# Where a kernel's scattered rows are issued, when its expert tiles start, and how far attention outputs are buffered

## The reference, cut to what matters

```python
x = x + tanh(g_xattn[0]) * xattn(layernorm(x), ctx, ctx, Wq, bq, Wk, bk, Wv, bv, Wo, bo, mask)
x = x + tanh(g_ffn[0]) * ffn(layernorm(x), gate_w, gate_b, w1, b1, w2, b2)
# xattn: softmax(q k^T / sqrt(8), masked) v, then @ Wo.T + bo
# ffn:
scores = x_flat @ gate_w + gate_b
topk_vals, topk_idx = top_k(scores, 2)
topk_probs = softmax(topk_vals)
combine_w = zeros((T, 8)).at[tok, topk_idx].add(topk_probs)
h = relu(einsum('td,edf->etf', x_flat, w1) + b1[:, None, :])
y = einsum('etf,efd->etd', h, w2) + b2[:, None, :]
out = einsum('te,etd->td', combine_w, y)
```

## Time and profile before

| | us |
|---|---|
| median of 3 runs | 507.41 (505.67 to 509.38) |
| the profiled execution | 506.01 |
| its span, first to last instruction | 504.2 |

### The profile page before, as it was taken

How to read it: one execution, slowest core, us unless ns; L and a number is a source line. 1 busy time by engine, 2 the same in 40 slices (tenths; PEclk the granted TensorE clock), 3 DMA queues, 4 the chain that set the end, 5 groups by cost and what they waited for, 6 DMA issues and landing times.

```text
span 504.2 us, 12347 instructions
## 1 busy us (share of the span) xinstructions
PE 418.4 (83%) x4299; PEld 333.3 (66%) x4299; DVE 268.6 (53%) x1010; ACT 284.4 (56%) x848; POOL 271.8 (54%) x297
## 2 busy tenths in 40 slices
PE   0779889999899999998988777988589999999900
PEld 0455667667667667576756466977479899999800
DVE  1345667777677676776667553433422333233247
ACT  1277868778787778786856711423133444444334
POOL 8536319059498496793942801864755355554500
PEclk9979999999999999999989956998879999999965
DMA  3999999500000000000010052555538677778278
GB/s 74 240 359 410 412 392 216 104 12 14 23 12 23 25 12 23 13 13 29 8 33 14 33 179 81 175 167 168 173 117 251 197 218 233 239 217 247 90 231 280
DMA packets 48155, 72.55 MB, mean 144 GB/s; under 512 B 8054, under 2 KB 32638, under 8 KB 48094
## 3 DMA queue, kind: packets, MB, share of 16 engines
q1 hardware_dynamic: 43549, 62.32, 40.6%
q0 software_dynamic: 4544, 9.45, 5.3%
HBM read 41.83 MB, written 34.66 MB: 152 GB/s over the span
## 4 chain that ended last, share of the span: by engine, by line
PE 74%; issue 8%; DVE 5%; DMA 4%; ACT 3%; SPq 3%; POOL 1%; another core or an unknown queue 1%; DVEq 0%; POOLq 0%; ACTq 0%
PE S L740 7%; PE T L718 7%; PE O L740 7%; PE U L718 7%; PE S L624 6%; PE O L664 6%; PE O L654 6%; PE T L632 6%; PE S L614 5%; PE U L632 5%; ACT P L819 2%; DMA yg<-res 2%; DVE PT L1074 2%; PE E L673 2%; PE E L688 2%
## 5 line engine op out<-in xcount | busy, mean ns | idle before, releaser
L819 ACT ACTIVATE P<-S,nmax 128x120 f32<-128x120 f32 x512 | 135.2, 420 | 6.9 <-DVE nmax L1068 5.4
L959 POOL DMA_INDIRECT zs<-z,posu x64 | 63.2, 988 | 99.6 <-DVE posu L1147 81.0
L970 POOL DMA_INDIRECT res<-yo,dpos x78 | 75.0, 961 | 64.7 <-DVE yo L1231 56.6
L1068 DVE TENSOR_REDUCE nmax<-S 128x4 f32<-128x480 f32 x128 | 75.1, 649 | 37.4 <-PE S L624 32.3
L826 ACT COPY PT<-U 120x512 f32<-120x512 f32 x64 | 39.6, 619 | 52.9 <-PE U L632 51.7
L856 ACT ACTIVATE H<-T,wbuf 128x256 f32<-128x256 f32 x78 | 32.7, 471 | 62.5 <-PE T L718 45.0
L614 PE MATMUL S<-mb_r,I_r 128*128 128x480 f32 x128 | 65.3, 514 | 2.1 <-ACT P L819 1.9
L856 ACT ACTIVATE H<-U,wbuf 128x256 f32<-128x256 f32 x78 | 32.7, 471 | 51.7 <-PE U L718 37.3
L938 POOL TENSOR_SCALAR Kb<-Kt,hm 128x480 f32<-128x480 f32 x32 | 47.0, 1482 | 18.2 <-ACT Kt L840 18.2
L928 POOL TENSOR_SCALAR z<-X,mv,rstd 128x128 f32<-128x128 f32 x64 | 50.2, 791 | 3.0 <-POOL rstd L923 2.7
L1080 DVE RECIPROCAL orec<-O 128x128 f32<-128x128 f32 x32 | 30.6, 957 | 39.2 <-PE O L664 39.2
(11 more groups left out here) (161 smaller groups left out, 654.0 us busy)
## 6 DMA issues: line engine op xcount, KB each, us to landing
wbuf<-wpk SPq DMA_DIRECT2D x39, 578.0 KB
zs<-zero SPq DMA_DIRECT2D x1, 17952.0 KB, 60.2
zin<-zs SPq DMA_DIRECT2D x39, 132.0 KB
yg<-res SPq DMA_DIRECT2D x16, 256.0 KB, 4.2
wpk<-in_w SPq DMA_DIRECT2D x1, 2048.0 KB, 57.7
wpk<-in_w SPq DMA_DIRECT2D x8, 256.0 KB, 9.3
out<-X SPq DMA_DIRECT2D x16, 128.0 KB, 3.4
ctx_sb<-in_ctx SPq DMA_DIRECT2D x1, 1440.0 KB, 16.8
```

The costliest lines, as they stand in the source:

```text
L819: ins = nc.scalar.activation(P[:, n % 4, j, :], a[:, j * LK:(j + 1) * LK], ACT.Exp, bias=nmax[:, n % 4, j:j + 1])
L959: nc.gpsimd.indirect_dma_start(out=zs, out_offset=bass.IndirectOffsetOnAxis(ap=posu[:, F, k, i:i + 1], axis=0), in_=z2[:, F % 2, i, :], in ...
L970: nc.gpsimd.indirect_dma_start(out=res, out_offset=bass.IndirectOffsetOnAxis(ap=dpos[:, n % NDP, h:h + 1], axis=0), in_=yo[:, n % NYO, h, ...
L1068: v.tensor_reduce(nmax[:, n % 4, :], Sb[n % NHG][:, 0:HG * LK].rearrange("p (j k) -> p j k", j=HG), AX_X, ALU.max, negate=True).then_inc(m ...
```

## The change

- `SCATTERS` issues a group's eight scatters as four at p = 1 and four at p = 3, both of group G - 2; none goes to the group after. Each part waits until the sums of batch k - 1 are done (`behind_sums`).
- From group 6 on, and for every scatter to `res`, a scatter also waits for `yo` number 4t/5 - 1, t being its turn (`paced`). Group 6's are issued in rounds 33 to 36, and the norm of `z2` for group 7 in round 33 instead of 34.
- Routing parts 4 and 5 stand ahead of the unload, part 2 of the table in round p = 2 instead of 3.
- `OT` has two buffers, `NYO` is 10.
- The steps of the tiles start in round 32, the opening steps at the end of round 31.
- SP loads tiles' rows and weights in turn, rows first; the wait for the table moves to the rows.

```diff
--- before.py
+++ after.py
@@ -35,8 +35,8 @@
 FIRST = ("Z", "C", "K", "Q", "V")
 
 
-SCATTERS = {0: (-3, (2, 3)), 1: (-2, (0,)), 2: (-2, ()), 3: (-2, (1,))}
-LAST_SCATTERS = {0: (), 1: (0,), 2: (1, 2), 3: (3,)}
+SCATTERS = {0: (-2, ()), 1: (-2, (0, 1)), 2: (-2, ()), 3: (-2, (2, 3))}
+LAST_SCATTERS = {0: (), 1: (0, 1), 2: (2,), 3: (3,)}
 
 
 
@@ -66,7 +66,7 @@
 NTAB = 13
 
 ZW, Z_TOK, Z_EXP = D + 4, D, D + 1
-NYO = 6
+NYO = 10
 NDP = NYO + 4
 
 TRASH = 2 + NDP * TS
@@ -94,7 +94,7 @@
 
     subs, pre, k = {}, {}, 0
     for b in range(NB):
-        j, k = 0, max(k, GB * (LAST[b] + 1) + 5)
+        j, k = 0, max(k, GB * (LAST[b] + 1) + 4)
         if k < NR:
             pre[k - 1] = b
         while j < SUBS[b] and k < NR:
@@ -304,7 +304,7 @@
         P = sb("P", [128, 4, HG, LK])
         PT = sb("PT", [LK, NPT, HG * LQ])
         orec = sb("orec", [128, LQ])
-        OT = sb("OT", [128, TOK])
+        OT = sb("OT", [128, 2, TOK])
         xb = sb("xb", [128, GB, D])
 
         z2T = sb("z2T", [128, TOK])
@@ -511,8 +511,6 @@
             def load_w(n):
 
                 b, i = tile_of(n)
-                if i == 0:
-                    sp.wait_ge(table_step, NTAB * (b + 1))
                 wait(sp, yo_done, TH * (n - NW + 1))
                 e = sp.value_load(tab[0:1, b, 1, i:i + 1], min_val=0, max_val=NE - 1)
                 sp.dma_start(wbuf[:, n % NW, :], wpk[bass.ds(e, 1)].squeeze(0)).then_inc(w_in[n % NW], 16)
@@ -521,6 +519,7 @@
 
                 b, i = tile_of(n)
                 if i == 0:
+                    sp.wait_ge(table_step, NTAB * (b + 1))
                     for q in range(2):
                         sp.wait_ge(scat[q], 16 * 2 * GB * ((LAST[b] + 1 - q) // 2))
                 if n >= NZ:
@@ -550,12 +549,13 @@
                     known = N0[b + 1]
                     if b + 1 < NB and ROUND_OF.get((b, 2 * TH * (i + 1) - 1), NEVER) > GB * (LAST[b + 1] + 1) + 1:
                         known = N0[b + 2]
-                    while w_next < min(N0[b] + i + NW, known):
-                        load_w(w_next)
-                        w_next += 1
-                    while z_next < min(N0[b] + i + NZ, known):
-                        load_z(z_next)
-                        z_next += 1
+                    while z_next < min(N0[b] + i + NZ, known) or w_next < min(N0[b] + i + NW, known):
+                        if z_next < min(N0[b] + i + NZ, known):
+                            load_z(z_next)
+                            z_next += 1
+                        if w_next < min(N0[b] + i + NW, known):
+                            load_w(w_next)
+                            w_next += 1
             stored(sp, N0[NB])
             for u in range(NU):
                 load_results(u)
@@ -670,7 +670,7 @@
                 a = entry("PROJ", G)
                 pe.wait_ge(o_free, at(G, GB, GB) + 1)
                 for i in range(GB):
-                    last = mm(a[:, i * D:(i + 1) * D], OT[:, i * LQ:(i + 1) * LQ], wo_sb[:], start=True, stop=True)
+                    last = mm(a[:, i * D:(i + 1) * D], OT[:, G % 2, i * LQ:(i + 1) * LQ], wo_sb[:], start=True, stop=True)
                 last.then_inc(e_ready, 1)
 
             def z2_entry(F):
@@ -945,6 +945,18 @@
                 nc.gpsimd.tensor_tensor(xb[:], group_x(G), bo_sb[:].unsqueeze(1).broadcast_to((128, GB, D)),
                                         ALU.add).then_inc(xb_done, 1)
 
+            def behind_sums(k):
+
+                if 1 <= k <= B:
+                    pool.wait_ge(pv_done, k)
+
+            turn = {"next": 0}
+
+            def paced():
+
+                turn["next"] += 1
+                return (turn["next"] - 1) * 4 // 5 - 1
+
             def scatter(F, part, parts):
 
                 if part == 0:
@@ -956,6 +968,8 @@
                     for k in range(2):
                         if (2 * i + k) * parts // (2 * GB) != part:
                             continue
+                        if F >= SB0[1]:
+                            wait(pool, yo_done, paced())
                         nc.gpsimd.indirect_dma_start(
                             out=zs, out_offset=bass.IndirectOffsetOnAxis(ap=posu[:, F, k, i:i + 1], axis=0),
                             in_=z2[:, F % 2, i, :], in_offset=None).then_inc(scat[F % 2], 16)
@@ -966,7 +980,7 @@
                 if q is None:
                     return
                 n, h = N0[b] + q // TH, q % TH
-                pool.wait_ge(yo_done, TH * N0[b] + q + 1)
+                pool.wait_ge(yo_done, max(TH * N0[b] + q + 1, paced()))
                 nc.gpsimd.indirect_dma_start(
                     out=res, out_offset=bass.IndirectOffsetOnAxis(ap=dpos[:, n % NDP, h:h + 1], axis=0),
                     in_=yo[:, n % NYO, h, :], in_offset=None).then_inc(y_out[n % NYO], 16)
@@ -974,17 +988,21 @@
             def round_(k):
                 G, p = divmod(k, GB)
                 F, parts = SCATTERS[p]
-                if 0 <= G + F < NG and G + F + 1 not in LAST:
+                if 0 <= G + F < NG and G + F + 1 not in LAST and k <= B:
                     for part in parts:
+                        behind_sums(k)
                         scatter(G + F, part, GB)
-                if p == 2 and 0 <= G - 1 < NG:
+                if p == (2 if G < NG else 1) and 0 <= G - 1 < NG:
                     pool.wait_ge(ln2_step, at(G - 1, 2, 2))
                     rstd(mv2, rstd2, rstd2_done, G - 1)
                     if G >= 3:
                         pool.wait_ge(scat[(G - 1) % 2], 16 * 2 * GB * ((G - 1) // 2))
                     normalise(z2[:, (G - 1) % 2, :, 0:D], G - 1, mv2, rstd2, z2_done, rstd2_done)
+                if B < k <= B + GB:
+                    scatter(NG - 2, k - B - 1, GB)
                 if G - 1 in LAST:
                     for part in LAST_SCATTERS[p] if G < NG else range(GB) if p == 1 else ():
+                        behind_sums(k)
                         scatter(G - 2, part, GB)
                 if p == 2 and G + 1 < NG:
                     masked_keys(G + 1)
@@ -1079,9 +1097,9 @@
                 G, i = divmod(k, GB)
                 v.reciprocal(orec[:], Ob[:, LQ:2 * LQ]).then_inc(orec_done, 1)
                 dve.wait_ge(orec_done, k + 1)
-                if i == 0 and G >= 1:
-                    ready(dve, "PROJ", G - 1)
-                v.tensor_tensor(OT[:, i * LQ:(i + 1) * LQ], Ob[:, 0:LQ], orec[:], ALU.mult).then_inc(o_free, 1)
+                if i == 0 and G >= 2:
+                    ready(dve, "PROJ", G - 2)
+                v.tensor_tensor(OT[:, G % 2, i * LQ:(i + 1) * LQ], Ob[:, 0:LQ], orec[:], ALU.mult).then_inc(o_free, 1)
 
             def residual(G):
                 ready(dve, "PROJ", G)
@@ -1258,6 +1276,8 @@
                         row_max(NHG * k + g)
                 if p < 2 and first:
                     taken[first[0]](first[1])
+                if 0 < p < 3 and 0 <= G - 2 < NG:
+                    route(G - 2, 4 if p == 1 else 5)
                 if 0 <= k - 1 < B:
                     unload(k - 1)
                 step(ks[1:2])
@@ -1265,8 +1285,8 @@
                     copy_pt(NHG * k)
                 if middle:
                     taken[middle[0]](middle[1])
-                if p < 3 and 0 <= G - 2 < NG:
-                    route(G - 2, {0: 2, 1: 4, 2: 5}[p])
+                if p == 0 and 0 <= G - 2 < NG:
+                    route(G - 2, 2)
                 if p == 1 and G - 2 == NG - 1:
                     route(G - 2, 5)
                 step(ks[3:4])
@@ -1280,7 +1300,6 @@
                 step(ks[7:8])
                 if p == 2 and G - 1 in LAST and G < NG:
                     table(sb_of(G - 2), 1)
-                if p == 3 and G - 1 in LAST and G < NG:
                     table(sb_of(G - 2), 2)
                 if k in PRE:
                     for i, _ in OPENING:
```

## The result

The changed kernel took 511.98 us (median of 20 runs) beside 508.86 us for the kernel before in the same job: ratio 1.0065, 95% interval 1.0046 to 1.0084. It is slower by 0.7%, where 484 us, 5% faster, was forecast. Two later jobs that ran it again gave 1.0072 (1.0038 to 1.0106) and 1.0051 (1.0013 to 1.0089). The ratios leave out single executions far above the rest, such as one of the kernel before at 745.77 us.

What follows compares the result with a forecast made beforehand. TensorE (PE) was taken to bound the kernel, with holes in its stream beside runs of scatters. Terms 9.1 + 1.4 + 3.1 + 0.8 + 2.4 + 7.3 - 2.2 took 21.9 off 506.01 us: 484 us, range 466 to 500.

Steps and rivals of the forecast that it cites:

- (a): Attention rounds: scatters as fours behind sums remove the holes of rounds 28 and 31, 9.1 us off, and small stalls, 1.4.
- (e): Tile stage: pacing scatters leaves one run of 12 to 20, costing 10 us instead of 17.3: 7.3 off.
- (f): SP's loads, z before w: tile 15's weights wait behind tile 16's z, 2.2 us lost.
- runs of four still hurt: Attention: four smaller stalls, 2.8 us in all, worth 0 to 2.8 because fours remain; half taken, 1.4 off.
- the second rival: Attention and tiles: fourteen fours cost 0.65 us each, tiles keep their 17.3: 499 us, 492 with half; chance 0.20.
- slower: Attention: fours behind sums delay transposes, scores and exponentials; at 2.1 us each, 511 us, slower by 1%; chance 0.05.
- (b): Attention unload: a doubled OT ends DVE's wait for PROJ, 0.45 us in each of 7 groups: 3.1 off.
- (c): Attention: routing parts 4 and 5 before the unload cost nothing; round 29 gains about 0.8 us.
- (d): Between attention and tiles: first product of H at T + 20.0 instead of T + 23.3; 2.4 us off.
- The pace works from the start: Tile stage: backlog short or PE keeps speed, 17.3 us gained and loads cost nothing: 472 us; chance 0.27.
- The holes are not the scatters': Whole kernel: holes come from how PE gets instructions, so moving scatters leaves them: 500 us; chance 0.07.

Runs made afterwards that it cites:

- e3: Changed kernel with two scatters behind each round's sums in four rounds, instead of four in two of them: 505.84 us, ratio 0.9900 to the kernel before.
- e5: Changed kernel with group 7's norm moved behind round 33's results, on a chip without the delay: 478.99 us, ratio 1.0040 to the kernel before.
- e17: Kernel before with only a memset of 335 columns added behind every scatter: 480.91 us, ratio 1.0109 to the kernel before.
- e18: e13 with the memset behind group 7's scatters too, on a third chip: 480.24 us, ratio 1.0078 to the kernel before.
- e2: Changed kernel with SP's load order of before (weights first, table's wait at the weights): 511.72 us, ratio 1.0004 to the kernel before.
- e1: Changed kernel without both waits for the scatters' pace: 514.16 us, ratio 1.0069 to the kernel before.
- e13: e11 plus a memset of 335 columns behind scatters of results and of groups 5 and 6: 481.70 us, ratio 0.9475 to the kernel before.
- e10: e5's kernel run again, on the chip with the delay: 504.54 us, ratio 0.9938 to the kernel before.
- e8: Changed kernel with groups 0 to 4's fours halved to 64 rows into an unread table, whole scatters added a round later: 515.23 us, ratio 1.0797.
- e11: e6's kernel run again, on the chip with the delay: 495.97 us, ratio 0.9785 to the kernel before.
- e6: Changed kernel with two scatters per round, loads' order of before, group 7's norm later, no pace in block 1: 474.42 us, ratio 0.9968 to the kernel before.
- e16: e11 with block 1's scatters paced as in the changed kernel: 490.03 us, ratio 0.9641 to the kernel before.
- e9: Changed kernel run again, unedited, on the chip with the delay: 510.41 us, ratio 1.0072 to the kernel before.
- e4: Changed kernel with a memset of 200 columns behind each scatter, scatters 1.41 us apart: 506.81 us, ratio 0.9937 to the kernel before.
- e14: e7's kernel run again, on the chip with the delay: 499.77 us, ratio 0.9842 to the kernel before.
- e7: Changed kernel with a memset of 335 columns behind each scatter, on a chip without the delay: 495.95 us, ratio 1.0395 to the kernel before.

## Why the prediction was wrong, step by step

The reading of the kernel before was right. I put its holes beside scatters at 17.3, 9.1 and 2.8 us, 29 in all. The same kernel takes 476 us on two chips and 507 to 511 on the one with the delay, 31 to 35 more. The error lies in where the change leaves them. Three steps failed: the price of a run of four in (a), the price of a long run and of the pace in (e), and the size of the wait in (f). From 21.9 off to 5.8 on, the profiled pair, are 27.7 us: about 10 in (a), 12 in block 0, 5 at the change of block and in block 1, 1 at the start of the tiles.

**(a) Scatters behind sums, forecast 10.5 off.** Round 28 and the sums of batch 30 came out as said (7.20 instead of 11.83, and values and sums 1.95 instead of 6.82). The step that failed is "runs of four still hurt", priced inside the sums alone at half of 0.65. Beside transposes, scores and exponentials a four costs 1.1 us at p = 3 and 0.9 at p = 1, as the windows of 8.76 and 9.29 against e3's 7.63 and 8.35 show. That runs only change place is what the second rival said, and its 0.65 was too low as well. Five rounds of the one and four of the other are 9.2 us, and rounds 29 and 30 add 1.8 and 1.1 (9.31 and 8.75 against 7.56 and 7.70 in e5): 12 us, more than the whole term. The way it happens, behind the sums at transposes, scores and copies, is that of the rival "slower", which got 0.05. It asked for a price of about 2 us in all fourteen rounds with everything else as summed; measured are 1.1 in eleven. The kernel came out slower because the tiles went wrong too.

**(b) OT doubled, forecast 3.1 off: right.** The waits of OT for PROJ (6.0 us in 7 times) are gone, and e17 against e18, on one chip, gives 0.60 us in each of five rounds (9, 13, 17, 21, 25), 3.0; round 5 adds another 0.6. No run doubles OT without the moved routing, so these hold both. In the changed kernel the delay of the fours hides most of it: 9.29 against 9.58 before.

**(c) Routing earlier, forecast 0.8 off.** No run separates it.

**(d) The start of the tiles, forecast 2.4 off:** 1.6. The first product of H came at T + 21.7 instead of T + 20.0. PE waited for rows twice, 4.71 and 2.77 us, near the 7 forecast as one wait.

**(e) Spaced scatters, forecast 7.3 off.** The run after the norm was computed as 12 to 20 long and is 16. Its price failed: 16 at 0.62 are 10 us, and the steps of 3.45, 13.07 and 3.67 us cost 14.6, low clock included. The mean price was taken from runs of 7, 8 and 13, and a long run costs more each: in the kernel before the steps beside these three already cost 1.6, 4.8 and 11.0 us above their due, 0.22, 0.60 and 0.84 a scatter, and the 16 cost 0.91. The next sentence failed as well: "the pace is five in 7.46 us with at most two close together: 0". Each double turn is followed by three or four turns at 1.27, and block 1 lost 4.1 us that it had not lost before. What I took from block 1 before, that 46 scatters at a mean of 1.88 us are harmless, holds for even spacing and not for the same mean in bursts.

**(f) SP loads z before w, forecast 2.2 lost.** The mechanism is as said, tile 15's weights behind tile 16's z; the size was a step of 9.20 us instead of 1.87, 7.3 lost. The landing was put at PE's need with the steps at full speed and POOL on time. e2 takes this wait away and regains 3 us, as its way from T to the first product of H is 24.7 us instead of 21.7. On the chip without the delay it is the one large loss left. Block 0's balance is then 14.6 and 7.3 against the 17.3 of before; the other 2.5 us are smaller, among them the first three steps, which have banks U and O alone (2.12, 2.09 and 2.76 us).

**The rivals.** The pace works from the start: no, the paced kernel has a row of 16, and without the pace the time is the same (e1). The holes are not the scatters': no, spacing the scatters takes the holes away (e3, e13) and a shorter run halves its hole (e10). Between 330 and 358 us, around PE's stop of 9.85, the trace also has no packet on the instruction queue q8. The Trainium skill, Runtime: NRT & Kernel Launch, Instruction fetch mechanics, holds such fetches to be mostly hidden; the trace agrees.

Not settled is how a scatter holds up the others. All engines stop, each behind work that had ended. The DMA engines are busy in the first third of the stop and mostly idle in the rest, as two windows show; the third line is their busy share in 40 slices from 344 to 346 us:

```profile
337.80:341.00 3.20, 0.00 (x0) 0.00 (x0) 0.00 (x0) 0.33 (x1) 2.48 (x3) 0.77 0.75 229
341.00:347.60 6.60, 0.00 (x0) 0.00 (x0) 0.43 (x3) 0.00 (x0) 3.82 (x4) 0.50 0.23 71
DMA  9952000000000000000000002997200000000000
```

e5's row of twenty moves 226 GB/s and e13's spaced row 182 without a stop. So the amount of data moved is not it. The Trainium skill's Perfetto Trace Analysis (DMA Instruction — SWDGE (GPSIMD)) says that the time shown for such an instruction is the writing of its descriptors, not the transfer. By that the 0.96 us that recur every 1.27 are descriptor writing. That this writing loads something which semaphores pass too is a guess; no run here shows it, nor why one chip of three has the delay. Whether the number of rows or of instructions counts is open as well (e8).

## What to carry to other kernels

Space the indirect scatters of a queue evenly (twos with gaps, or a short memset behind each), and judge a pace by the distances it leaves after a double turn, not by its mean. Do not put a load that waits for late work ahead of loads that early work needs in one queue. And time a kernel on more than one chip before a gain from spacing is believed: e13 is 5.3% faster than the kernel before on one chip, and its nearest relative e18 is 0.8% slower on another; of the three edited kernels timed on both kinds of chip only e11 (e6 there) is faster on both, 2.2% and 0.3%.

## What the runs showed of the hardware

- On one of the three chips of the five jobs, indirect scatters 1.27 us apart hold up PE, ACT and DVE: four of them by about 1.1 us, a row of 16 by 14.6 us with the low clock behind it. A row of 20 does nothing on another. On the third no row this close was traced; there the kernel before took 476.4 us, as on the second. One program took 504.5 us on the one and 479.0 on another (e10, e5).
- Where the delay is, it has a sharp edge in spacing: at 1.27 us a row of ten costs 6.6 to 7.8 us (e16, e10, e11) and one of 16 costs 14.6 to 15.4 (the changed kernel, e9); at 1.41 a row of 17 still costs 14.7 (e4); at 1.52 a row of 18 costs 0.8 (e13) and one of 36, about 25 of them beside steps, costs 1.6 (e14).
- It grows faster than the row: 7, 8, 13 and 16 scatters in a row cost 1.6, 4.8, 11.0 and 14.6 us.
- With scatters 1.52 us apart the chips differ little: 499.8 and 496.0 us for one program (e14, e7).
